# Softmax row sums from a column of ones in the value product, and the product in two banks

## What is computed

```python
qm = split_heads(q @ Wq.T + bq)      # 16 heads of 32
km = split_heads(k @ Wk.T + bk)      # 128 context rows
vm = split_heads(v @ Wv.T + bv)
scores = einsum('bnlh,bnph->bnlp', qm, km) / sqrt(32)
attn = softmax(where(mask, scores, MASK_FILL), axis=-1)
out = einsum('bnlp,bnph->bnlh', attn, vm)
return out @ Wo.T + bo
```

## Time and profile before

| | |
|---|---|
| median of 3 runs | 2012.2 us (2003.86 to 2014.26) |
| the profiled execution | 2007.3 us, its span 2005.5 us |
| PE busy | 1740.6 us (87%), weight loads 1427.7 us (71%) |
| DVE busy | 1617.7 us (81%) |
| ACT busy | 960.2 us (48%), of it 361.6 in 1024 exponentials and 235.6 in 1024 accumulator reads |
| GpSimd busy | 1128.5 us (56%) |
| mean granted TensorE clock | 0.950 of full |

### The profile page before, as it was taken

The page is one execution under the profiler, slowest core; times in us unless marked ns, Lnnn a source line. Parts: engine busy times, 40 slices in busy tenths (PEclk is TensorE's granted clock), DMA queues, the critical chain, the costliest instruction groups (busy, mean ns, idle before and its releaser), DMA issues.

```text
span 2005.5 us, 39950 instructions
## 1 busy us (share of the span) xinstructions
PE 1740.6 (87%) x14016; PEld 1427.7 (71%) x14016; DVE 1617.7 (81%) x2433; ACT 960.2 (48%) x3070; POOL 1128.5 (56%) x857
## 2 busy tenths in 40 slices
PE   5789999999988888894699988898988989889984
PEld 4677777777777777783477777777777777777763
DVE  6598888888888888887378888788887888878875
ACT  4222211222222221211368777777777777777772
POOL 0387778776776777785344555344653446534422
PEclk8899999999999999997699999999999999989987
DMA  7101111111111001103111110111101111011101
GB/s 238 62 1 43 42 42 42 42 42 42 42 42 39 19 26 42 42 21 122 43 40 45 56 61 17 56 56 56 61 17 56 56 56 61 23 51 56 34 23 42
DMA packets 55157, 98.11 MB, mean 49 GB/s; under 512 B 5184, under 2 KB 12480, under 8 KB 54976
## 3 DMA queue, kind: packets, MB, share of 16 engines
q1 hardware_dynamic: 53104, 94.12, 13.9%
q10 hardware_dynamic: 1872, 1.66, 0.3%
HBM read 58.80 MB, written 36.96 MB: 48 GB/s over the span
## 4 chain that ended last, share of the span: by engine, by line
PE 29%; DVE 14%; issue 5%; ACT 3%; POOL 1%; DVEq 1%; POOLq 0%; ACTq 0%
PE ring L1119 18%; PE sc L1147 4%; PE ring L1214 3%; DVE ntop L1324 3%; ACT prob_c L1251 2%; DVE stats_c L1362 2%; DVE x2T L1291 2%; DVE stats L1331 1%; PE sc L1139 1%; PE ring L1124 1%; PE ring L1172 1%; DVE x L1345 1%; DVE pT L1291 1%; DVE x L1381 1%; ACT x2T L1224 1%
## 5 line engine op out<-in xcount | busy, mean ns | idle before, releaser
L510 PE MATMUL qb<-wqkv,xT 128*128 128x512 f32 x2304 | 556.5, 398 | 8.0 <-DVE qk L692 5.7
L510 PEld LDWEIGHTS qb<-wqkv,xT 128*128 128x128 f32 x2304 | 433.7, 191 | 108.9 <-DVE qk L692 12.5
L1251 ACT ACTIVATE prob_c<-sc,ntop 128x128 f32<-128x128 f32 x1024 | 361.6, 390 | 142.7 <-DVE ntop L1324 142.7
L1074 POOL TENSOR_TENSOR rstd<-vare,half_c 128x1 f32<-128x1 f32 x64 | 35.0, 547 | 454.5 <-DVE vare L1338 454.5
L604 ACT ACTIVATE aT<-tb 128x512 fp32r<-128x512 f32 x64 | 36.5, 589 | 473.2 <-PE tb L518 473.2
L1119 PE MATMUL ring<-wqkv,aT_c 128*128 128x512 f32 x768 | 202.1, 414 | 39.7 <-DVE x L1345 39.7
L1251 ACT ACTIVATION_READ_ACCUMULATOR prob_c<-sc,ntop 128x1 f32 x1024 | 235.6, 230 | 0.0
L588 PE MATMUL ob<-wout,aT 128*128 128x512 f32 x768 | 200.0, 412 | 34.6 <-DVE aT L768 32.7
L1324 DVE TENSOR_REDUCE ntop<-sc 128x4 f32<-128x512 f32 x256 | 170.2, 688 | 39.1 <-PE sc L1147 25.5
L1119 PEld LDWEIGHTS ring<-wqkv,aT_c 128*128 128x128 f32 x768 | 145.6, 197 | 75.5 <-DVE x L1345 36.0
L588 PEld LDWEIGHTS ob<-wout,aT 128*128 128x128 f32 x768 | 145.9, 196 | 67.4 <-DVE aT L768 22.5
(11 more groups left out here) (128 smaller groups left out, 3448.5 us busy)
## 6 DMA issues: line engine op xcount, KB each, us to landing
x_tile<-in_x SPq DMA_DIRECT2D x16, 1024.0 KB, 7.3
x_scratch<-xres SPq DMA_DIRECT2D x16, 1024.0 KB, 5.4
x_tile<-x_scratch SPq DMA_DIRECT2D x16, 1024.0 KB, 6.8
out<-x SPq DMA_DIRECT2D x64, 256.0 KB, 2.0
kt<-k_scratch SPq DMA_DIRECT2D x16, 512.0 KB, 3.2
v_c<-v_scratch SPq DMA_DIRECT2D x16, 256.0 KB, 4.0
raw<-in_wqkv SPq DMA_DIRECT2D x3, 1024.0 KB, 16.8
ctx<-in_ctx SPq DMA_DIRECT2D x1, 1024.0 KB, 7.6
```

What stands on the lines that cost most here:

```text
L510: last = nc.tensor.matmul(qb[g % 4][:, :], xT[p][a][:, k, t * P:(t + 1) * P], wqkv[b][:, k, c * D:(c + 1) * D], start=(n == 0), stop=(n == ...
L1251: last = nc.scalar.activation(prob[:, h, :], sc[g][:, (h % 4) * C:(h % 4 + 1) * C], ACT.Exp, bias=ntop[:, h:h + 1], accum_out=total[:, t % ...
```

## The change

The two low/high parts of v get a 33rd column per head: ones in the high part, zeros in the low part (`vparts`, `v_c`, and the scratch tensor's row of 1024 elements of which VW = 528 are used per part). The value product then gives the row sum in column 33 of each head. As 16 x 33 columns don't fit into a bank, a tile's product takes two ring turns of 8 heads each. The exponentials lose `accum_out`. DVE takes two reciprocals of 8 sums from the banks and multiplies in two halves. The store of v in the preparation becomes four DMAs, and the load of v alone now waits for the value products of the step before.

```diff
+VW = H * (DH + 1)
...
-        vparts = sb("vparts", [P, R, 2, D], F16)
+        vparts = sb("vparts", [P, R, 2, H, DH + 1], F16)
...
-            sp.dma_start(v_dram.rearrange("r c a n -> c r (a n)"),
-                         vparts[:, :, :, :].rearrange("p r a n -> p r (a n)")).then_inc(kv_out, 16)
-            sp.wait_ge(kv_out, 16 * (2 * R + 2))
+            sp.wait_ge(v_sums, 2)
+            for r in range(R):
+                sp.dma_start(v_dram[r, :, :, 0:VW],
+                             vparts[:, r, :, :, :].rearrange("p a h d -> p a (h d)")).then_inc(kv_out, 16)
+            sp.wait_ge(kv_out, 16 * (3 * R + 1))
...
+            nc.vector.memset(vparts[:, :, 0, :, DH:DH + 1], 1.0).then_inc(v_sums, 1)
+            nc.vector.memset(vparts[:, :, 1, :, DH:DH + 1], 0.0).then_inc(v_sums, 1)
...
 def slot_turns(t):
-    turns = [("out", t), ("pv", t)]
+    turns = [("out", t), ("pv", 2 * t), ("pv", 2 * t + 1)]
...
-    "pv": lambda j, i: 4 * j + i,
+    "pv": lambda j, i: 8 * j + i - 1,
...
-                wait_each(sp, (scored, 16 * j), (psum["pv"], 4 * (j - 1)))
+                wait_each(sp, (scored, 16 * j))
...
-                sp.dma_start(v[:, p, :, :], v_flat[bass.ds(rows[0], P), :, :]).then_inc(v_in[p], 16)
+                wait(sp, psum["pv"], 8 * (j - 1))
+                sp.dma_start(v[:, p, :, :, :].rearrange("c a h d -> c a (h d)"),
+                             v_flat[bass.ds(rows[0], P), :, 0:VW]).then_inc(v_in[p], 16)
...
-                        dst = bank(j, p, ("pv", t))
-                        for h in range(H):
-                            head = slice(head_of(h) * DH, (head_of(h) + 1) * DH)
-                            for n, (a, b) in enumerate(PASSES):
-                                last = nc.tensor.matmul(dst[:, head], pT[a][:, h, :], v[:, pp, b, head],
-                                                        start=(n == 0), stop=(n == 2))
-                        last.then_inc(psum["pv"], 1)
+                        for half in range(2):
+                            dst = bank(j, p, ("pv", 2 * t + half))
+                            for h in range(H // 2):
+                                slot = half * (H // 2) + h
+                                for n, (a, b) in enumerate(PASSES):
+                                    last = nc.tensor.matmul(dst[:, h * (DH + 1):(h + 1) * (DH + 1)], pT[a][:, slot, :],
+                                                            v[:, pp, b, head_of(slot), :], start=(n == 0), stop=(n == 2))
+                            last.then_inc(psum["pv"], 1)
...
-                            if g == 0:
-                                wait(act, taken["pv"], 4 * j + t - 1)
...
-                                                            ACT.Exp, bias=ntop[:, h:h + 1],
-                                                            accum_out=total[:, t % 2, head_of(h):head_of(h) + 1])
+                                                            ACT.Exp, bias=ntop[:, h:h + 1])
...
-                        wait(dve, exped, 4 * over)
-                        wait(dve, taken["pv"], over - 1)
-                        nc.vector.reciprocal(rtotal[:, :], total[:, (t - 1) % 2, :]).then_inc(summed, 1)
-                        wait(dve, summed, over)
-                        wait(dve, psum["pv"], over)
-                        wait(dve, psum["aT"], over - 1)
-                        nc.vector.tensor_tensor(attn[:, :].rearrange("p (h d) -> p h d", d=DH),
-                                                ring[bank_of(p, ("pv", t))][:, :].rearrange("p (h d) -> p h d", d=DH),
-                                                bcast(rtotal[:, :], DH), ALU.mult).then_inc(taken["pv"], 1)
+                        for half in range(2):
+                            wait(dve, psum["pv"], over[half])
+                            wait(dve, taken["pv"], over[half] - 2)
+                            nc.vector.reciprocal(rtotal[:, half, :], heads[half][:, :, DH]).then_inc(summed, 1)
+                        wait(dve, psum["aT"], 4 * j + t - 1)
+                        for half in range(2):
+                            wait(dve, summed, over[half])
+                            dst = attn[:, :].rearrange("p (m i d) -> p i m d", i=4, d=DH)[:, 2 * half:2 * half + 2, :, :]
+                            nc.vector.tensor_tensor(dst, heads[half][:, :, 0:DH].rearrange("p (i m) d -> p i m d", m=DK),
+                                                    rtotal[:, half, :].rearrange("p (i m o) -> p i m o", m=DK, o=1)
+                                                    .to_broadcast([P, 2, DK, DH]), ALU.mult).then_inc(taken["pv"], 1)
...
-               "v": nc.dram_tensor("v_scratch", [R, C, 2, D], F16).ap(),
+               "v": nc.dram_tensor("v_scratch", [R, C, 2, 2 * D], F16).ap(),
```

More of the change, by code:

```diff
@@ L130, in prepare_block @@
         v_trans, v_h, v_l = sem("v_trans"), sem("v_h"), sem("v_l")
-        kv_out, bias_ready = sem("kv_out"), sem("bias_ready")
+        kv_out, bias_ready, v_sums = sem("kv_out"), sem("bias_ready"), sem("v_sums")
         ident, wqkv, wout = keep["ident"], keep["wqkv"], keep["wout"]
@@ L243, in _ @@
                 act.wait_ge(v_trans, r + 1)
-                nc.scalar.activation(vparts[:, r, 0, :], pv[r][:, :], ACT.Copy).then_inc(v_h, 1)
+                nc.scalar.activation(vparts[:, r, 0, :, 0:DH], pv[r][:, :].rearrange("p (h d) -> p h d", d=DH),
+                                     ACT.Copy).then_inc(v_h, 1)
         @block.vector
@@ L303, in _ @@
                 dve.wait_ge(v_h, r + 1)
-                nc.vector.tensor_tensor(vparts[:, r, 1, :], pv[r][:, :], vparts[:, r, 0, :],
+                nc.vector.tensor_tensor(vparts[:, r, 1, :, 0:DH], pv[r][:, :].rearrange("p (h d) -> p h d", d=DH),
+                                        vparts[:, r, 0, :, 0:DH],
                                         ALU.subtract).then_inc(v_l, 1)
@@ L888, in active @@
 def active(j, kind, i):
-    shift = {"pv": -(i == 0), "aT": -(i == 0), "wo": -(i < 2), "x2T": -(i < 3), "pT": 0,
+    shift = {"pv": -(i < 2), "aT": -(i == 0), "wo": -(i < 2), "x2T": -(i < 3), "pT": 0,
              "xT": 1, "q": 1, "s": -1, "out": -2}[kind]
@@ L944, in cross_block @@
         fill = sb("fillrows", [P, C], F32R)
-        v = sb("v_c", [C, 2, 2, D], F16)
+        v = sb("v_c", [C, 2, 2, H, DH + 1], F16)
         x1 = keep["x_tile"]
@@ L962, in cross_block @@
         ntop = sb("ntop", [P, H])
-        total = sb("total_c", [P, 2, H])
-        rtotal = sb("rtotal", [P, H])
+        rtotal = sb("rtotal", [P, 2, H // 2])
         half = sb("half_c", [P, R])
@@ L1157, in step @@
                                              [wf[0][:, :, :], wf[1][:, :, :]])]).then_inc(psum["out"], 1)
-                    if active(j, "pv", t):
-                        over = TURNS_OVER["pv"](j, t)
+                    if active(j, "pv", 2 * t):
                         pp = p if t > 0 else 1 - p
-                        wait(pe, taken["pT"], 4 * over)
+                        wait(pe, taken["pT"], 4 * (4 * j + t))
                         if t == 1:
@@ L1196, in step @@
                     if active(j, "aT", t):
-                        wait(pe, taken["pv"], TURNS_OVER["pv"](j, t))
+                        wait(pe, taken["pv"], TURNS_OVER["pv"](j, 2 * t + 1))
                         transpose_tile(bank(j, p, ("aT", t)), attn).then_inc(psum["aT"], 1)
@@ L1272, in step @@
                     if has(j):
-                        wait(act, psum["pv"], 4 * j + t)
+                        wait(act, psum["pv"], 8 * j + 2 * t)
                         for g in range(4):
@@ L1346, in step @@
                                                 ALU.add).then_inc(taken["out"], 1)
-                    if active(j, "pv", t):
-                        over = TURNS_OVER["pv"](j, t)
-                        wait(dve, exped, 4 * over)
-                        wait(dve, taken["pv"], over - 1)
-                        nc.vector.reciprocal(rtotal[:, :], total[:, (t - 1) % 2, :]).then_inc(summed, 1)
-                        wait(dve, summed, over)
-                        wait(dve, psum["pv"], over)
-                        wait(dve, psum["aT"], over - 1)
-                        nc.vector.tensor_tensor(attn[:, :].rearrange("p (h d) -> p h d", d=DH),
-                                                ring[bank_of(p, ("pv", t))][:, :].rearrange("p (h d) -> p h d", d=DH),
-                                                bcast(rtotal[:, :], DH), ALU.mult).then_inc(taken["pv"], 1)
+                    if active(j, "pv", 2 * t):
+                        over = [TURNS_OVER["pv"](j, 2 * t + half) for half in range(2)]
+                        heads = [ring[bank_of(p, ("pv", 2 * t + half))][:, 0:VW // 2].rearrange("p (h d) -> p h d", d=DH + 1)
+                                 for half in range(2)]
+                        for half in range(2):
[9 more added lines that the diff above has]
```

(1 more changed line is left out.)

## The result

The changed kernel takes 2059.95 us (median of 4 runs, 2051.42 to 2061.44); the kernel before, with one more run beside it, 2008.29 (2003.86 to 2014.26). The ratio is 1.0246, with a 95% interval of 1.0202 to 1.0291: 52 us slower by the medians. The forecast was 2028, and its range ended at 2050.

What follows compares the result with a forecast made beforehand. No engine was free by share; the chain DVE, PE, ACT copy bound the steady slots. Handover 15.7, slot 0 1.6, slot 3 0.3, preparation 0.6 and edges -2.0 gave +16.2 us on the 2012.2 median: 2028, range 2014 to 2050.

Steps and rivals of the forecast that it cites:

- the ring's part: Cross stage, slots 1 and 2: wo waits for the first pv bank instead of "out"; 15.7 us over 13 steps.
- the sum of +16.2: Whole kernel: 15.7 handover, 1.6 slot 0, 0.3 slot 3, 0.6 preparation, -2.0 edges, in us.
- Clock falls: Rival, chance 0.20: longer stands before wo drop TensorE to 1.2 GHz; 2078 if in all 26 slots.
- The handover: Slots 1 and 2: out addition's start to wo's start 1.34 instead of 0.73, with the second reciprocal +0.68, bounds 0.61 and 0.89.
- In a third of them, 2045: Lighter form of the clock rival: the clock falls in a third of the 26 slots, total 2045 us.
- The relief: ACT, steps 2 to 14: removed accumulator reads, 92 us in all, lie beside other work and gain nothing.
- Steps 0 and 1: Edges: step 0, bound by exponentials, gains 2.2 us; step 1 loses 0.8 us.
- DVE in slot 0: Second half product and reciprocal are on the path: 0.2 us in 8 of 13 steps, 1.6 in all.
- Slot 3: Bound by PE: 33 columns for 32 in 48 matmuls per tile add 0.02 us, 0.3 in all.
- The preparation: Last store becomes four: +0.6 us, bounds 0 and +1.0.
- Step 16: Tail of the cross stage: wo waits for an older turn instead of "out", -1.5 us.
- the signs listed: Trace signs for right or wrong: ACT idle up some 80 us, wo waiting for attn_c in about 28 places, slot 1 at 12.9.

Runs made afterwards that it cites:

- filler run: Changed kernel with five more 512-column matmuls in each slot 1 and 2, where TensorE waits for the out addition: 2026.39 us, ratio 1.0086.
- later out addition: Kernel before with one more DVE addition of 512 columns ahead of the out addition in slots 1 and 2 of steps 2 to 15: 2065.69 us, 1.0278.
- reciprocals first: Changed kernel with both reciprocals moved ahead of DVE's out addition: 2054.67 us, ratio 1.0208.
- the new order: Changed kernel with DVE's out addition, reciprocals and products ahead of maxima of groups 2 and 3, ACT's xT copies ahead of group 2's exponentials: 2001.24 us.
- take between: Changed kernel with DVE's out addition, reciprocals and half products moved ahead of the row maxima of group 3 only: 2009.90 us, ratio 0.9994.
- early take: Changed kernel with DVE's out addition, reciprocals and half products moved ahead of the row maxima of groups 2 and 3: 2005.87 us, ratio 0.9974.
- reads put back: Changed kernel with the exponentials' accumulator reads put back, their results not used: 2063.87 us, ratio 1.0270.
- sums from the accumulator: Changed kernel with 32-column value products in two banks, row sums from the exponentials' accumulator and one reciprocal from SBUF: 2073.15 us, 1.0312.

## Why the prediction was wrong

The direction, the ring's part and its size were right. The step that failed is the clock: the sum of +16.2 has no term for it, the rival *Clock falls* was given 0.20, and what was set against it, "the longest single stand would be 1.2 to 1.4", was wrong. The stand was 1.70, the clock fell in 18 of 26 slots, and that cost 26.0 us.

- **The handover.** Forecast +0.68, measured 1.38 - 0.73 = +0.65. Slots 1 and 2 at full clock are 0.53 and 0.68 longer, which are the two figures of the sum: 15.7 us.
- **Its pieces.** A half product was put at 0.42 and two reciprocals 0.07 apart. Measured (ns, minimum, median, maximum):

```profile
L1365 DVE TENSOR_TENSOR attn_c<-ring,rtotal x128: 379/417/426, 1005.7 to 2016.9; 128x256 f32<-128x256 f32 x128
```

```profile
L1360 DVE RECIPROCAL rtotal<-ring x128: 153/196/208, 1005.4 to 2016.5; 128x8 f32<-128x8 f32 x128
```

  The half product took 0.417. (0.60 for 512 columns is 0.85 columns per ns, not the 0.96 that I read from it; the full and the half product differ by 0.275 for 256, which is 0.93, so the 0.42 came out all the same.) And both reciprocals take 0.27 together against 0.24 for the one, which in the kernel before is

```profile
L1352 DVE RECIPROCAL rtotal<-total_c x64: 240/242/245, 997.3 to 1963.8; 128x16 f32<-128x16 f32 x64
```

  The Trainium skill (VectorE: DVE Perf Modes, The TRN2 errata) charges more for a source in PSUM; an estimate by its cycles is 133 ns for 8 columns there against 77 for 16 in SBUF. The rows have 196 from the bank and 242 from SBUF: they don't agree, and what the page would have added was rightly left out of the sum (65 ns for each of two reciprocals in 34 slots is 4.4 us, not the 2 that I wrote). The page's other formula there, (N + 151) / 0.96 ns for a float32 tensor_tensor addition, gives an estimate of 424 for the half product, and the 417 agrees.
- **The stand before wo.** It was 1.28 us in one piece, behind two transposes. I split the new one, 1.95, around "one tile of transposes" and took 1.2 to 1.4 for its longer part. But that second tile used to run ahead of the stand; held back by the out bank, it leaves its place as idle time: 1.70. And the row that I set against the rival, steady slots that hold the clock at 1.28, said nothing about 1.7 or 1.9. The rows for the other side, 2.15 and 2.57, were as near. And the trace of before has the clock falling inside the loop too, in slot 0 behind each of the loop's returns, where PE had stood over 3 us (step 7; the window's clock is 0.50):

```profile
1403.04 0.80 PE L1139 MATMUL sc<-fillrows,ones 32*128 32x512 f32 x4 [3.31 <-issue]
...
1409.01 4.15 PE L1119 MATMUL ring<-wqkv,aT_c 128*128 128x512 f32 x12
```

```profile
1403.00:1405.00 2.00, 1.97 (x32) 1.89 (x36) 0.00 (x0) 0.00 (x0) 0.00 (x0) 0.50 0.06 16
```

  I used these returns for DVE's slot 0 alone.
- **Its price.** I had 1.9 us for a slow wo, from the last steps; in the loop it is 1.44 (14.33 on average against 12.90): the clock falls inside the product, or in the transposes just ahead of it. It happened 18 times of 26, so 26 us. The filler run removes just this, and the later out addition brings it into the kernel before: shown, not argued. "In a third of them, 2045" was the right form with the wrong share: 15.7 + 26 on 2008.3 is 2050, and of what is left to 2060 the ledger has most ahead of the cross stage.
- **The relief.** Cost at nothing in the steady part: right, to 0.01 us per slot. Steps 0 and 1 were to give 1.4 us net and gave 1.0, with one slow wo in them.
- **DVE in slot 0** was to be 0.2 longer and is 0.09. Slot 3 was to be 0.02 longer and is 0.07 shorter. **The preparation**: +0.6 forecast, some 1.2 measured: the four stores took 2.69 us to issue, not 1.4, and landed in 3.3.
- **Step 16** was to gain 1.5. PE did stand 0.88 before wo instead of 2.57, but the wo before it ran slow (4.24); step 15 and the rest are 3.0 us longer.
- Of the signs listed, these came: no accumulator reads, slot 1 at 12.9 and slot 2 longer by 0.7 at full clock, a wait before the second xT for the out addition. That wait was to be the short one, and a wait before wo for attn_c was to come in about 28 places: the first is the whole stand, 1.70 us in each slot, and the second came in 5 places, none in steps 2 to 14. ACT's idle before the exponentials and before x2T was to grow by some 80 us and grew by 113 (142.7 + 66.3 to 159.8 + 162.1): ACT lost 82 us of work, and the kernel is 54 longer. "wo products over 3.1 us in the loop" was named as what would show the forecast wrong, and it did in slots 1 and 2; as worded it would not have told the kernels apart, since before has four of them, all in slot 0 behind a loop return.

What stays open: which of the 26 slots the lower clock hits in a run, and so how many. Slots that agree to 0.02 us up to wo differ in it, and with the reciprocals first (1.84 ahead of xT instead of 1.70, wo 0.1 earlier) the number was the same 18.

## What to carry to other kernels

In a ring of banks the order of turns is a set of waits: a product that takes one turn more moves every wait behind it to another, later taker, and that has to be read off turn by turn before the saving on the relieved engine is counted. Time taken off an engine that is not on the chain is only room. A change of order may use it, but then run the order without the change as well: here the new order undid the loss and won 9 us more (2060 to 2001), and in two slots of the kernel before it did as much by itself (2001). Where TensorE stands before a long product, price a longer stand twice, by its length and by that product's rows at the lower clock; draw the new timeline before you split a stand into pieces; and when the trace has rows for a short and a long stand only, give the case in between its even chance.

## What the runs showed of the hardware

- Where TensorE stood 1.28 (before), 1.09 (take between) or 0.51 us (early take) in slots 1 and 2, all 26 wo products of these kernels ran at 2.4 GHz. With 1.70 us before four transposes wo was slow in 18 (changed) or 20 of 26 (reads put back; sums from the accumulator), with 1.84 in 18, with 2.2 to 2.6 in one piece in 15. Five matmuls in the stand, whose rest was then 0.50, brought that to none.
- The length of the stand alone does not decide a single slot. In the changed kernel's step 1, PE stood 2.06 us before wo and wo took 3.05; in the next slot it stood 1.92 and wo took 4.59. With the early take, both stands of step 15 were 1.59, and wo took 3.03 and 4.58.
- An accumulator read occupies ACT for 0.09 us although its row says 0.19 to 0.31. Exponentials of 128 columns follow each other in 0.34 with it and in 0.25 without (medians; four take 1.14). By the Trainium skill (ScalarE: Activation LUTs, What ACT_TABLE_LOAD costs) an estimate is 0.387 less 0.093 of overlap, 0.29; the measurement is shorter.
- A 128x512 addition of two SBUF operands that are the same tile took 1.02 us on DVE, where a subtraction of two different ones takes 0.68. Why was not tried.
- In the two-bank kernel with sums from the accumulator, the trace has waits for three semaphores between the reciprocal and the half product on DVE's queue, and it starts 0.44 us after the reciprocal. In the kernel before there is one, and the full product starts 0.28 after. No run varies this alone.
